# Tile 0 picked from ten groups in two halves, the count one conv block earlier, tile 1's row found apart, and a new order on VectorE

## The reference, cut to what matters

```
x = x + tanh(g_xattn) * hyena(layernorm(x), k, bias, ctx, ctx)     # stage 1: a causal convolution per head pair
h = layernorm(x)
logits = h @ router_w                                              # 8 experts
e = argmax(logits);                                                # top 1, 2048 rows in all
y = (silu(h @ gate_w[e]) * (h @ up_w[e])) @ down_w[e]              # 512 -> 1024 -> 512
out = x + tanh(g_ffn) * y
```

## Time and profile before

| | us |
|---|---|
| median of three executions | 695.22 |
| lowest and highest of them | 689.46, 696.67 |
| the profiled execution, its own time | 686.31 |
| its span in the profile | 684.6 |
| PE busy | 649.9 (95%) |
| DVE busy | 523.7 (76%) |
| POOL busy | 547.4 (80%) |
| ACT busy | 236.2 (35%) |

### The profile page before, as it was taken

One profiled execution on the slowest core, in us unless ns is written; L12 is line 12 of the kernel. 1 busy time (PEld: TensorE's weight loads), 2 busy tenths in 40 slices (PEclk: granted clock), 3 DMA queues, 4 the chain that ended last, 5 costly groups with the idle time before them and its releaser, 6 DMA issues.

```text
span 684.6 us, 10887 instructions
## 1 busy us (share of the span) xinstructions
PE 649.9 (95%) x3188; PEld 533.6 (78%) x3189; DVE 523.7 (76%) x658; ACT 236.2 (35%) x344; POOL 547.4 (80%) x353
## 2 busy tenths in 40 slices
PE   4959999999999999999999899999999999999994
PEld 4748888888888888778788588888888888888873
DVE  6797888888888888699999947799999929541510
ACT  4523333343444444342223133223333233332320
POOL 2977999999999999948378658888888878775842
PEclk9979999999999999999999899999999999999998
DMA  7335555555555555568676646366676645440110
GB/s 222 112 136 168 187 175 183 172 183 182 189 178 180 172 184 167 200 218 293 206 226 216 214 145 212 115 208 217 227 220 200 214 155 184 129 146 33 45 49 18
DMA packets 51906, 117.77 MB, mean 172 GB/s; under 512 B 5900, under 2 KB 6092, under 8 KB 51888
## 3 DMA queue, kind: packets, MB, share of 16 engines
q1 hardware_dynamic: 43728, 99.68, 45.5%
q0 software_dynamic: 4320, 12.72, 5.4%
q10 hardware_dynamic: 3840, 5.15, 2.7%
HBM read 94.08 MB, written 25.02 MB: 174 GB/s over the span
## 4 chain that ended last, share of the span: by engine, by line
PE 75%; DVE 13%; issue 6%; POOL 4%; ACT 1%; DMA 1%; DVEq 0%; SPq 0%; POOLq 0%
PE pair L1385 26%; PE bank L1290 25%; PE bank L1401 14%; PE pair L1320 3%; PE bank L1416 2%; DVE prod L1127 2%; POOL kv_lo L710 2%; PE pair L1260 2%; DVE up L1204 1%; POOL prod L727 1%; PE pair L1301 1%; DVE gate L1204 1%; DVE kv L1057 1%; PE bank L1361 1%; DVE up L1207 1%
## 5 line engine op out<-in xcount | busy, mean ns | idle before, releaser
L1290 PE MATMUL bank<-kv_hi,strip 128*128 128x512 f32 x640 | 214.1, 404 | 1.2 <-DVE kv_lo L1082 0.7
L710 POOL TENSOR_TENSOR kv_lo<-kv,kv_hi 128x2048 fp32r<-128x2048 f32 x31 | 144.2, 4653 | 7.1 <-ACT kv_hi L876 7.0
L1290 PEld LDWEIGHTS bank<-kv_hi,strip 128*128 128x128 f32 x640 | 122.0, 191 | 28.6 <-DVE kv_lo L1082 1.1
L1290 PE MATMUL bank<-kv_lo,strip 128*128 128x512 f32 x320 | 126.9, 397 | 0.0
L1095 DVE TENSOR_TENSOR prod<-bank,cT 128x512 f32<-128x512 f32 x128 | 85.1, 684 | 24.7 <-PE bank L1290 24.5
L876 ACT ACTIVATE kv_hi<-kv 128x2048 fp32r<-128x2048 f32 x31 | 59.5, 1920 | 118.8 <-DVE kv L1057 99.5
L1385 PE MATMUL pair<-gate,xT_hi 128*128 (+1 forms) x288 | 92.0, 400 | 2.2 <-issue 2.2
L1385 PE MATMUL pair<-up,xT_hi 128*128 (+1 forms) x288 | 90.4, 395 | 0.0
L1057 DVE TENSOR_TENSOR kv<-pair,cK 128x2048 f32<-128x2048 f32 x31 | 70.7, 2281 | 1.8 <-PE pair L1260 1.2
L1290 PEld LDWEIGHTS bank<-kv_lo,strip 128*128 128x128 f32 x320 | 61.2, 191 | 12.0
L727 POOL TENSOR_TENSOR prod<-prod 128x2048 f32<-128x2048 f32 x14 | 64.6, 4614 | 3.2 <-DVE prod L1095 3.2
(11 more groups left out here) (184 smaller groups left out, 1158.8 us busy)
## 6 DMA issues: line engine op xcount, KB each, us to landing
raw<-gate_w SPq DMA_DIRECT2D x32, 512.0 KB, 3.9
raw<-down_w SPq DMA_DIRECT2D x32, 512.0 KB, 3.7
strip<-kparts SPq DMA_DIRECT2D x15, 1024.0 KB, 5.9
raw<-up_w SPq DMA_DIRECT2D x28, 512.0 KB, 3.9
sorted_x<-fill SPq DMA_DIRECT2D x14, 792.0 KB, 4.7
xs<-sorted_x ACTq DMA_DIRECT2D x19, 256.5 KB, 2.8
x_in<-x_back SPq DMA_DIRECT2D x16, 256.0 KB, 4.8
cK<-ctx_back SPq DMA_DIRECT2D x16, 256.0 KB, 5.0
```

Source lines behind the costliest of these rows:

```text
L710: nc.gpsimd.tensor_tensor(kv_lo[u][:, hh, :], kv[:, hh, :], kv_hi[u][:, hh, :].bitcast(f32), ALU.subtract).then_inc(s_klo, 1)
L1290: last = nc.tensor.matmul(y_bank[lb][:, :], strip[u][:, 2 * hh + t, d * P:(d + 1) * P], v[u][:, hh, mb * COL:(mb + 1) * COL], start=(mb == ...
```

## The change

- `chosen` holds GS = 10 groups instead of 14. Tile 0 is picked from the first ten groups only. Rows of expert 0 in groups 10 to 13 are shifted to position 128 or later, should the first ten groups hold fewer than 128 (`kept`, `shift`).
- `count_first` also counts the ten groups (10 small matmuls more into `taken_bank`) and stands before conv block 1 of the last half instead of after it.
- DVE does `places_first` right after `product(1,0)`, ahead of `ln2_first(G-2)`. It has 16 steps and a cast instead of 13 and a cast.
- `sum_heads(G-1)` sums five terms (0, 1, 2, 3 and the skip term) instead of three; `add_fours(G-1)` is gone.
- The last picked group goes in two halves into two banks, and the high and low parts of tile 0 are made half by half. The gate projection starts with the first half's low part. 3 filler transposes stand where 12 did.
- Tile 1's row in `sorted_x` is worked out in `places_last` (`at_one`, semaphore `s_one`), so `load(1)` doesn't wait for the table.
- DVE: tile 0's low parts and `places_last` come right after `pick_experts`, before the gate's last low part; the four up low parts follow, then the table; all four chunks of the first down matrix are split after `hid` and `xT_lo`.

```diff
@@ placement and counting
+    GS = G - 6
-    chosen = put("chosen", [P, G1, P], f32, [down_at])
+    chosen = put("chosen", [P, GS, P], f32, [down_at])
+        taken_bank = v_bank[:, (G1 + 1) * E:(G1 + 2) * E]
@@ def count_first(pe):
+            for g in range(GS):
+                last = nc.tensor.matmul(taken_bank, ones_b[:, :], hot[:, g, :], start=False, stop=(g == GS - 1))
             last.then_inc(s_cnt, 1)
@@ def places_first(dve):
+            step(dve, n + 1, V.tensor_scalar(kept[:, :], taken_bank[:, 0:1], float(P), None, ALU.max))
+            step(dve, n + 2, V.tensor_tensor(shift[:, :], kept[:, :], taken_bank[:, 0:1], ALU.subtract))
+            step(dve, n + 3, V.tensor_copy(first_n[:, 1:E], total_bank[:, 1:E]))
+            step(dve, n + 4, V.tensor_tensor(first_n[:, 0:1], total_bank[:, 0:1], shift[:, :], ALU.add))
...
-            step(dve, n + 4, V.tensor_scalar(room[:, 0:1], room[:, 0:1], float(SPARE + 1), None, ALU.max))
...
+            step(dve, n + 12, V.tensor_scalar(mine[:, GS:G1, 0:1], mine[:, GS:G1, 0:1], shift[:, 0:1], None, ALU.add))
...
-            step(dve, n + 11, V.tensor_copy(first_n[:, :], total_bank))
-            step(dve, n + 12, V.tensor_scalar(first_n[:, 0:1], first_n[:, 0:1], float(P), None, ALU.max))
-            step(dve, n + 13, V.tensor_tensor(next_at[:, :], first_n[:, :], base_e[:, :], ALU.add))
+            step(dve, n + 15, V.tensor_tensor(next_at[:, :], first_n[:, :], base_e[:, :], ALU.add))
+            step(dve, n + 16, V.tensor_scalar(to_one[:, :], base_e[:, 1:2], -1.0, float(P), ALU.mult, ALU.add))
@@ def places_last(dve):
+            step(dve, n + 4, V.tensor_scalar(past_one[:, :], total_last[:, 0:1], first_n[:, 0:1], float(P), ALU.add,
+                                             ALU.is_gt))
+            V.tensor_scalar(at_one[:, :], past_one[0:1, :], to_one[0:1, 0:1], base_e[0:1, 1:2], ALU.mult, ALU.add)\
+                .then_inc(s_one, 1)
@@ ACT
-                act.wait_ge(s_xtr, 1)
-                nc.scalar.activation(flat(xT_hi_first), x_bank[:, :], ACT.Copy).then_inc(s_xT, 1)
+                for n, (turned, done) in enumerate(((s_xtr0, s_xT0), (s_xtr, s_xT))):
+                    act.wait_ge(turned, 1)
+                    nc.scalar.activation(half_of(xT_hi_first, n), picked[n][:, 0:L // 2], ACT.Copy)\
+                        .then_inc(done, 1)
...
-                act.wait_ge(s_tab, 1)
+                act.wait_ge(s_one, 1)
                 load(1)
@@ DVE, the last stage
                     product(g, u, n, 1, 0)
+                    if final:
+                        places_first(dve)
                     if before:
                         ln2_first(g - 1, 1 - u)
                         ln2_last(g - 1)
                     product(g, u, n, 1, 1)
-                    if final:
-                        places_first(dve)
                     product(g, u, n, 1, 2)
@@ DVE, after the stages
                 add_last_pairs(G - 1, 1)
-                add_fours(G - 1, 1)
                 first_low_parts(dve, GATE, range(1))
...
-                choose(dve, range(7, G1))
+                choose(dve, range(7, GS))
                 first_low_parts(dve, GATE, range(1, CH - 1))
                 pick_experts(dve, 1, G1, G)
+                for n, (high, done) in enumerate(((s_xT0, s_xlo0), (s_xT, s_xlo))):
+                    dve.wait_ge(high, 1)
+                    nc.vector.tensor_tensor(half_of(xT_lo_first, n), picked[n][:, 0:L // 2],
+                                            half_of(xT_hi_first, n).bitcast(f32), ALU.subtract).then_inc(done, 1)
+                places_last(dve)
                 first_low_parts(dve, GATE, range(CH - 1, CH))
-                places_last(dve)
-                first_low_parts(dve, UP, range(CH - 1))
-                dve.wait_ge(s_xT, 1)
-                nc.vector.tensor_tensor(flat(xT_lo_first), x_bank[:, :], flat(xT_hi_first).bitcast(f32),
-                                        ALU.subtract).then_inc(s_xlo, 1)
-                first_low_parts(dve, UP, range(CH - 1, CH))
+                first_low_parts(dve, UP, range(CH))
                 tile_table(dve)
...
-                split_matrix(DOWN, 0, 2, range(CH - 1))
                 dve.wait_ge(s_silu, 1)
...
-                split_matrix(DOWN, 0, 2, range(CH - 1, CH))
+                split_matrix(DOWN, 0, 2)
@@ PE
-                    terms = [0, 1, J]
+                    terms = [0, 1, 2, 3, J] if isinstance(g, int) and g == G - 1 else [0, 1, J]
...
-                    conv(g, u, n, 1, (0, 1))
+                    conv(g, u, n, 1, (0,))
                     if isinstance(g, int) and g == G - 1:
                         count_first(pe)
-                    conv(g, u, n, 1, (2, 3))
+                    conv(g, u, n, 1, (1, 2, 3))
...
+                        if first == GATE and b == LB // 2:
+                            pe.wait_ge(s_xlo, 1)
...
-                take(range(8, 9))
+                take(range(8, GS - 1))
+                take(range(GS - 1, GS), range(LB // 2), s_xtr0)
                 count_last(pe)
-                take(range(9, G1))
-                keep_busy(12)
+                take(range(GS - 1, GS), range(LB // 2, LB), s_xtr)
+                keep_busy(3)
```

More of the change, by code:

```diff
@@ L102, in flamingo_layer_kernel @@
     tile_at = put("tile_at", [1, TILES + 2], i32)
+    at_one = put("at_one", [1, 1], i32)
     end_q = put("end_q", [1, E], i32)
@@ L191, in flamingo_layer_kernel @@
     next_at = put("next_at", [P, E], f32, table)
+    kept = put("kept", [P, 1], f32, table)
+    shift = put("shift", [P, 1], f32, table)
+    to_one = put("to_one", [P, 1], f32, table)
+    past_one = put("past_one", [P, 1], f32, table)
     n_tiles = put("n_tiles", [P, E], f32, table)
@@ L398, in places_first @@
+            step(dve, n + 5, V.tensor_tensor(over[:, :, 0:G1], first_n[:, :].unsqueeze(2).broadcast_to([P, E, G1]),
                                              bounds[:, 0:G1].unsqueeze(1).broadcast_to([P, E, G1]), ALU.is_gt))
-            step(dve, n + 2, V.tensor_reduce(n_first[:, :], over[:, :, 0:G1], AX, ALU.add))
-            step(dve, n + 3, V.tensor_scalar(room[:, :], n_first[:, :], float(SPARE), None, ALU.add))
-            step(dve, n + 4, V.tensor_scalar(room[:, 0:1], room[:, 0:1], float(SPARE + 1), None, ALU.max))
@@ L402, in places_first @@
-            step(dve, n + 5, V.tensor_tensor(past_n[:, :, :], room[:, :].unsqueeze(1).broadcast_to(ee),
+            step(dve, n + 6, V.tensor_reduce(n_first[:, :], over[:, :, 0:G1], AX, ALU.add))
+            step(dve, n + 7, V.tensor_scalar(room[:, :], n_first[:, :], float(SPARE), None, ALU.add))
+            step(dve, n + 8, V.tensor_tensor(past_n[:, :, :], room[:, :].unsqueeze(1).broadcast_to(ee),
                                              ahead[:, :, :], ALU.mult))
-            step(dve, n + 6, V.tensor_reduce(tiles_ahead[:, :], past_n[:, :, :], AX, ALU.add))
@@ L405, in places_first @@
[L405 to L409 removed]
+            step(dve, n + 9, V.tensor_reduce(tiles_ahead[:, :], past_n[:, :, :], AX, ALU.add))
@@ new lines, in places_first @@
+            step(dve, n + 10, V.tensor_scalar(base_e[:, :], tiles_ahead[:, :], float(P), None, ALU.mult))
+            step(dve, n + 11, V.tensor_tensor(mine[:, 0:G1, :], rank_bank.rearrange("p (g e) -> p g e", e=E),
+                                              base_e[:, :].unsqueeze(1).broadcast_to(ge), ALU.add))
+            step(dve, n + 12, V.tensor_scalar(mine[:, GS:G1, 0:1], mine[:, GS:G1, 0:1], shift[:, 0:1], None, ALU.add))
+            step(dve, n + 13, V.tensor_tensor(mine[:, 0:G1, :], mine[:, 0:G1, :], hot[:, 0:G1, :], ALU.mult))
@@ L508, in flamingo_layer_kernel @@
         x_bank, out_bank = psum[0], psum[1]
+        picked = (x_bank, out_bank)
         h_bank = psum[2:4]
@@ L959, in load @@
                         act.wait_ge(s_next, t)
-                    place = bass.ds(act.value_load(tile_at[0:1, blk(t)], min_val=0,
+                    at = at_one[0:1, 0:1] if isinstance(t, int) and t == 1 else tile_at[0:1, blk(t)]
+                    place = bass.ds(act.value_load(at, min_val=0,
                                                    max_val=(FILL * (G - 2) - 1) * P), P)
@@ L1363, in x_in_array, with take @@
                     last.then_inc(s_xtr, 1)
-                def take(groups):
+                def take(groups, blocks=range(LB), done=None):
                     for g in groups:
                         pe.wait_ge(s_choice, g + 1)
-                        for b in range(LB):
-                            last = nc.tensor.matmul(x_bank[:, b * P:(b + 1) * P], xn_all[:, g, b * P:(b + 1) * P],
-                                                    chosen[:, g, :], start=(g == 0 and b == 0),
-                                                    stop=(g == G1 - 1 and b == LB - 1))
-                    if g == G1 - 1:
-                        last.then_inc(s_xtr, 1)
+                        for b in blocks:
+                            n, c = divmod(b, LB // 2)
```

(5 more changed lines are left out.)

32 lines of the change are left out of this document (18 added, 14 removed).

## The result

The changed kernel takes 696.51 us (median of 20, 693.55 to 701.78), the kernel before, run beside it, 689.47 (median of 20, 686.50 to 696.67). The ratio is 1.0101, 95% interval 1.0081 to 1.0122: +7.0 us, where the sum had said +7.7. The measured 696.51 lies half a microsecond inside the lower end of the stated range of 696 to 708.

The account below looks back on a forecast made before the run. The prediction took DVE's weight splitting (about 332 to 391 us), and the seam between stages before it, to bound the kernel. First down matrix +6.4, +7.7 with the low clock, carried to the end: 695.2 + 7.7 = 702.9 us, range 696 to 708.

Parts of the forecast that it names:

- step 1: End of stage 1: positions cast at some 298.8 instead of 299.86; places_first takes 3.95 us instead of 3.34.
- step 2: Behind places_first: ln2_first(G-2) 4.4 us later, logits_of(G-2) on PE +3.25, POOL's first scatter 2.2 late.
- step 3: sum_heads(G-1) on PE: 20 instructions instead of 12, +0.91 us; sum ends 3.8 later, residual at 311.25.
- steps 4 and 6: Gate start on PE: 0.9 us sooner at full clock; low clock loses 2.5, giving 322.5 instead of 320.91.
- step 5: DVE to the first down matrix: silu 332.1 from 330.22, four chunks after hid; done +6.4 us at full clock.
- step 7: To the end: new PE wait of 4 to 6 us at the up matrix doesn't add; DVE's +7.7 carries over.
- Rival B: Lateness partly absorbed at the down matrix: +7.7 less 2.2 to 5, about 699 us; chance 0.15.
- C: Not slower: PE's own order, not DVE's stream, releases PE at the second expert; say 694.5 us; chance 0.12.
- D: Up matrix wait brings half clock, PE reaches tile 2's down after DVE; 7.7 + 3, 706 us; chance 0.12.
- A: Clock holds at 2.4 GHz around 302 us, leaving +6.4: 701.6 us; chance 0.20.

Follow-up runs that it names:

- e4: Kernel before with only the count and places_first moved one conv block sooner, ahead of the layer norm statistics: 682.82 us, ratio 1.0009.
- e2: Changed kernel, unedited, profiled again on another chip: 686.88 us, span - C = 391.1.
- e9: Changed kernel with a waited one-column copy ahead of each of the four up low parts: 689.28 us, ratio 1.0114.
- e3: Changed kernel with group 14's layer norm statistics put back ahead of places_first: 685.82 us, ratio 1.0087.
- e1: Kernel before, unedited, profiled again on another chip: 684.03 us, span - C = 383.0.
- e5: Changed kernel with three of four first down matrix chunks split before hid again: 699.08 us, ratio 1.0082.
- e8: Changed kernel with 11 and 20 filler transposes in PE's new idle time: 699.34 us, ratio 1.0143.
- e12: Changed kernel with the first group's head sum in five terms too: 694.13 us (median of 12), ratio 1.0033.
- e6: Changed kernel with layer norm statistics ahead of places_first and three down chunks before hid: 688.83 us, ratio 0.9948.
- e7: Same edits as e6 on the changed kernel, plus a waited copy ahead of each up low part: 681.92 us, ratio 0.9884.
- e11: Changed kernel with layer norm first, three down chunks ahead, waited copies, and five terms for the first group: 677.86 us, ratio 0.996.
- e10: Kernel before with the very first group's head sum in five terms on PE: 677.09 us, ratio 0.9956.

## Why the prediction was right

The size was right (+7.7 for +7.0 measured; by the traces without the pause 391.1 less the mean of 384.3 and 383.0: +7.5), and the reason for the start of it too. But two terms were wrong by 4 us each, with opposite signs; that the sum came out so close is luck.

1. *Count and places sooner* (step 1): as said; the scatters gained nothing by it.
2. *What it pushes back* (step 2): `logits_of(G-2)` +3.25 predicted, +3.5 measured, with PE waiting 2.38 for `xn2T`. First scatter +2.2 predicted, +3.5 measured: I had left out the 0.9 us from the end of the `xn_rows` copy to the scatter. e4 shows this step alone at +4.7.
3. *Five terms* (step 3): 20 instructions took 2.35, 12 took 1.53: +0.8 for +0.91. `residual` came +5.6, between the 3.8 without and the 6.3 with the low clock.
4. *The latency chain and the clock* (steps 4 and 6): gate +1.6 predicted (322.5 against 320.91), +0.5 in e2. The clock fell as in the earlier trace rows, to 0.57 from 300 to 304 us, but it was back at 1.00 from 304, while PE was picking: 1.6 us lost, not 2.5. (The 0.65 from `hot` to ACT's marker is counted from the start of `hot`; from its end it is 0.48.)
5. *DVE to the first down matrix* (step 5): the term that was mis-sized. The 332.1 there was silu +1.9; it was +5.2. I had moved the last scatters at their old price, while the new order laid five subtractions over one of them, and I had not dated the table. The table is done 6.7 later than before (C+25.9 and C+32.6), behind a `residual` that is 5.6 later, and silu can't start before it. By e9, where silu is 1.1 behind the table, the held scatter added at most 1.4 of the 5.2 in e2; the table alone would have made the rest. In e3, where the table is done at C+27.6, the held scatter is what comes last: load(1) at C+32.2, silu at C+34.1. `hid` came +4.3, the three chunks more behind it 5.6, and one of their copies took 2.89 instead of 0.69 (+2.2), beside POOL's `hT_lo`: +12.0 for +7.7.
6. *To the end* (step 7): the new wait at the up matrix came (4.8 us, 4 to 6 predicted). That DVE's splitting runs on to 391.32 + 7.7 failed, in the other direction: it made up 3.6 us on the way. DVE's groups from the end of the first down matrix to the end of expert 1's (columns: what, count, busy us and mean ns, idle us), before (336 to 392.5) and in e2 (341.7 to 394.7):

```profile
L1207 DVE TENSOR_TENSOR gate<-raw,gate 128x1024 fp32r<-128x1024 f32 x8 | 14.4, 1797 | 0.3
L1204 DVE CAST gate<-raw 128x1024 fp32r<-128x1024 f32 x8 | 7.7, 963 | 0.0
L1204 DVE CAST down_hi<-raw 128x1024 fp32r<-128x1024 f32 x4 | 3.8, 958 | 0.0
```
```profile
L1234 DVE TENSOR_TENSOR gate<-raw,gate 128x1024 fp32r<-128x1024 f32 x8 | 11.9, 1486 | 0.3
L1231 DVE CAST gate<-raw 128x1024 fp32r<-128x1024 f32 x8 | 5.5, 687 | 0.0
L1231 DVE CAST down_hi<-raw 128x1024 fp32r<-128x1024 f32 x4 | 5.0, 1238 | 0.0
```

Eight chunks are two matrices. The two gate matrices took 22.1 us before and 17.4 in e2, the down copies 1.2 more: 3.5 us given back. Most of it is one copy beside POOL's `hT_lo` of the first tile. Before, it fell in the gate matrix; in e2 it is the long copy of step 5, in the first down matrix. DVE and POOL before, then in e2:

```profile
337.94 2.89 DVE L1204 CAST gate<-raw 128x1024 fp32r<-128x1024 f32 x1
```
```profile
337.83 2.46 POOL L806 TENSOR_TENSOR hT_lo<-mid,hT_hi 128x1024 fp32r<-128x1024 f32 x1 [3.60 <-ACT mid L998]
```
```profile
335.89 2.89 DVE L1231 CAST down_hi<-raw 128x1024 fp32r<-128x1024 f32 x1
```
```profile
335.85 2.38 POOL L831 TENSOR_TENSOR hT_lo<-mid,hT_hi 128x1024 fp32r<-128x1024 f32 x1 [3.71 <-ACT mid L1026]
```

So 2.2 of the +12.0 only show where the date was taken. The other 1.3 go with PE's wait at the up matrix: POOL's `hid` waited 13.4 us for ACT in e2 and 4.7 before, and its work of the third tile came so late that one of the two subtractions which held DVE before the end of the down matrix (1.1 us) fell behind it.

```profile
L826 POOL TENSOR_TENSOR hid<-hid,mid 128x1024 f32<-128x1024 f32 x3 | 7.5, 2496 | 13.4 <-ACT mid L1015 13.4
```

So +12.0 became +8.4 at expert 1's down matrix (+8.0 against e1). From there to the end the first profile took 292.1, e1 290.4 and e2 290.5, and the end is +6.8 and +8.1, +7.5 in the mean. The first profile alone still ran at the low clock there, until 395.5. Rival B (partly absorbed) named the subtraction that fell behind the last chunk, but that is 1.1 us, where B took off 2.2 to 5. C fell: DVE's stream did release PE, and e3 shows that an earlier front doesn't bring the end forward by more than 1.1. D's half clock did come behind the new wait (0.68 from 360 to 364 us and 0.50 to 368 in e2), but its added loss at the down matrix didn't: PE waits there 0.3 us. A's sum was near, for the clock cost 1.6.

Taken back one after another, behind C: changed 391.1, layer norm first 390.0, down chunks first too 387.9, gaps too 385.1; before 383.0 to 384.3. Single undoings bring 1.1, 1.8 and 0.6 (e3, e5, e9; the 1.8 between two profiles with the pause), all three together 6.0. With one wait gone the next one in line ends last, as the table does in e9.

## What to carry to other kernels

When one wait on a chain of several engines is taken away, list who ends next and by how much; here undoing the costliest step alone (4.7 us by itself) brought 1.1 us. Before moving a GpSimd DMA or a block of two-input VectorE work, lay the two timelines over each other in the new order, and leave a waited step between long subtractions where a scatter must get in. If a kernel's times form clusters, compare profiles of both at the first date where they part: a race far from the change can move the median as much as the change does.

## What was not expected of the hardware

- *A scatter held over a whole run.* 0.97 us alone, 2.36 at most in the kernel before, 6.66, 6.16 and 5.77 over an unbroken run of subtractions, and 2.12 once four waited copies of 0.15 us stood in it. The Trainium skill (SBUF — State Buffer, the section "SBUF: two separate sides") says that GpSimd can't write the descriptors of its DMA while VectorE runs an operation in a 2-port performance mode, such as an fp32 copy. Here plain subtractions of two SBUF inputs do it, and in these three traces the hold wasn't given up between one subtraction and the next. In the kernel before one scatter did get in after the first of three (316.92, above), so the hold isn't certain.
- *A race worth 6 us.* Two additions of 1.2 us against one `kv_lo` of 4.6, at 37 us, decide whether an execution is a long or a short one. The starts ahead of it hardly differ: DVE's first addition and POOL's `vc` start at 36.91 and 37.26 in the first profile and at 36.69 and 36.88 in e1, both long, and at 36.74 and 36.88 in e4, which is short. DVE starts first in all three, but `vc` took 0.93, 0.90 and 1.86. So the recorded starts don't tell who gets the port at that point.
- *The pause.* In the profiles after, e5, e8 and e12, DVE's `residual` or ACT's `xn2T` starts 1.1 to 7.3 us after the end of the PE work that it needs, where it is 0.05 in e2, and PE is idle 2.9 to 6.5 us in all between C+15 and C+24 with no cause that the profile names. In each of the four the longest piece of that idle time ends 0.05 or 0.06 us after the ACT operation that PE needs next, so it follows from the late starts; the short pieces (0.4 to 2.9 us in all) remain. It isn't in e6 or e7, from the same chip as e5 and e8, nor in e1 to e4 or e9 to e11. All four profiles with it have the places ahead of the layer norm, and e5 and e6 differ in that alone; but e2, e4 and e9, on other chips, have that order too and no pause. PE's idle time just before it isn't the cause, as e8 fills it. On the chip of e5 to e8 all 25 runs of the kernel before took 687.4 to 696.3, where the chips of e1 and e10 gave 676.9 to 686.2; that is as if it fell there too, but no profile of the kernel before caught it. Its cause stays open.
